# q and k kept in memory by half blocks, with the four chunks of a row side by side

## The reference

```python
xn = _layernorm(x)                                   # 6250 x 512
qkv = (xn @ W_qkv.T + b_qkv).reshape(1, S, 8, 192)   # 8 heads of 64
q, k, v = split(qkv, 3, axis=-1)
q, k = sigmoid(q), sigmoid(k)
i = sum(q * sum(k, axis=1), axis=3)                  # norms, a number per token and head
o = sum(k * sum(q, axis=1), axis=3)
i_hat = sum(q * sum(k / o, axis=1), axis=3)          # scales
o_hat = sum(k * sum(q / i, axis=1), axis=3)
vw = v * softmax(o_hat, axis=1)
kv = einsum('bshd,bshe->bsde', k, vw)                # per token: heads against heads
r = einsum('bshd,bsde->bshe', q / i, kv) * sigmoid(i_hat)
mix = r.reshape(1, S, 512) @ W_out.T + b_out
gnn = xn + relu(concat(xn, segment_mean(edge_attr, dst)) @ W1 + b1) @ W2 + b2
x = x + gnn + mix
x = x + gate * (_layernorm(x) @ We[best] + be[best])
```

## Time and profile before

| | |
|---|---|
| median of the runs | 2144.1 us |
| profiled execution | 2139.87 us, span 2138.1 us |
| TensorE busy | 1876.4 us, 88%, mean granted clock 0.919 |
| VectorE busy | 1223.4 us, 57% |
| ScalarE busy | 561.3 us, 26% |
| GpSimd busy | 1323.2 us, 62% |
| DMA | 530000 packets, 400.77 MB, mean 187 GB/s |
| hardware queue | 407780 packets, 60.7% of 16 engines |
| scatter queue | 119952 packets, 21.3% of 16 engines |

### The profile page before, as it was taken

The page is one execution under the profiler, slowest core; times in us unless marked ns, Lnnn a source line. Parts: engine busy times, 40 slices in busy tenths (PEclk is TensorE's granted clock), DMA queues, the critical chain, the costliest instruction groups (busy, mean ns, idle before and its releaser), DMA issues.

```text
span 2138.1 us, 31097 instructions
## 1 busy us (share of the span) xinstructions
PE 1876.4 (88%) x10776; PEld 1511.0 (71%) x10776; DVE 1223.4 (57%) x3872; ACT 561.3 (26%) x1314; POOL 1323.2 (62%) x850
## 2 busy tenths in 40 slices
PE   2799999999999999788765888878776999998798
PEld 1688888888888888544435777667664888887586
DVE  3643454443444332277755756566558888885575
ACT  1422333223333223111131221212122433343210
POOL 4888888888888888688888888888881000000100
PEclk9999999999999999866586988889887999999899
DMA  8977887877777677899799999999977766653884
GB/s 289 224 159 149 140 157 147 168 153 133 156 155 154 131 131 147 204 219 214 145 293 189 210 173 216 174 206 200 179 150 219 215 212 218 211 186 114 309 296 150
DMA packets 530000, 400.77 MB, mean 187 GB/s; under 512 B 356900, under 2 KB 394020, under 8 KB 529844
## 3 DMA queue, kind: packets, MB, share of 16 engines
q1 hardware_dynamic: 407780, 369.74, 60.7%
q0 software_dynamic: 119952, 28.99, 21.3%
q10 hardware_dynamic: 2112, 0.07, 0.1%
HBM read 244.05 MB, written 154.62 MB: 186 GB/s over the span
## 4 chain that ended last, share of the span: by engine, by line
PE 67%; SPq 17%; DVE 6%; DMA 5%; issue 3%; ACT 1%; POOL 0%; DVEq 0%; POOLq 0%; ACTq 0%
PE pr_out_bank L359 26%; PE gn_acc L359 12%; SPq L1333 8%; PE pr_v_bank L359 7%; PE edge_sum L243 6%; PE ex_y_bank L359 6%; SPq L1349 3%; PE at_acc L359 2%; PE nm_io_bank L854 1%; DVE nm_wide L1052 1%; SPq L190 1%; DMA done<-qk_T 1%; PE gn_h L1906 1%; DVE edge_sel L231 1%; PE gn_h L1907 1%
## 5 line engine op out<-in xcount | busy, mean ns | idle before, releaser
L291 POOL DMA_INDIRECT table<-edge_ring,edge_row x831 | 1312.0, 1579 | 292.7 <-issue 231.5
L231 DVE SCALAR_TENSOR_TENSOR edge_sel<-edge_dst_all,edge_dst_f,upper 128x128 f32<-128x128 int16 x831 | 317.4, 438 | 93.3 <-PE edge_sum L243 84.3
L359 PE MATMUL pr_out_bank<-pr_norm_xT_hi,pr_w_hi 128*128 128x512 f32 (+1 forms) x832 | 327.6, 394 | 0.0
L359 PE MATMUL pr_out_bank<-pr_norm_xT_lo,pr_w_hi 128*128 128x512 f32 (+1 forms) x832 | 319.3, 384 | 0.0
L359 PE MATMUL pr_out_bank<-pr_norm_xT_hi,pr_w_lo 128*128 128x512 f32 (+1 forms) x832 | 318.6, 383 | 0.0
L243 PEld LDWEIGHTS edge_sum<-edge_attr,edge_sel 128*128 128x128 f32 x1662 | 237.5, 213 | 112.1 <-DVE edge_sel L231 78.9
L243 PE MATMUL edge_sum<-edge_attr,edge_sel 128*128 128x65 f32 x1662 | 245.1, 297 | 74.6 <-DVE edge_sel L231 69.1
L2247 POOL DMA_INDIRECT ex_w_raw<-in_w_exp,ex_row x4 | 5.4, 1341 | 371.6 <-issue 371.6
L256 ACT ACTIVATE edge_ring<-edge_sum 128x260 f32<-128x260 f32 (+1 forms) x209 | 80.5, 385 | 408.3 <-PE edge_sum L243 320.7
L359 PEld LDWEIGHTS pr_out_bank<-pr_norm_xT_lo,pr_w_hi 128*128 128x128 f32 x832 | 156.6, 188 | 32.2
L359 PEld LDWEIGHTS pr_out_bank<-pr_norm_xT_hi,pr_w_lo 128*128 128x128 f32 x832 | 157.1, 189 | 28.3
(11 more groups left out here) (206 smaller groups left out, 3217.6 us busy)
## 6 DMA issues: line engine op xcount, KB each, us to landing
edge_dst_all<-dst SPq DMA_DIRECT2D x103, 256.0 KB
edge_attr<-in_edge_attr SPq DMA_DIRECT2D x103, 256.0 KB
qk_T<-pr_stage SPq DMA_DIRECT2D x48, 512.0 KB
h_pre_T<-pr_stage SPq DMA_DIRECT2D x48, 512.0 KB
gn_pre<-h_pre_T SPq DMA_DIRECT2D x48, 512.0 KB, 6.4
done<-qk_T SPq DMA_DIRECT2D x16, 1024.0 KB
table<-edge_ring,edge_row POOLq DMA_INDIRECT x831
pr_norm_x<-in_x SPq DMA_DIRECT2D x12, 1024.0 KB
```

What stands on the lines that cost most here:

```text
L231: op = dve.scalar_tensor_tensor(out=self.sel[q][0:rows, j, 0:rows], in0=self.dst_all[k][0:rows, t:t + m * (rows - 1) + 1:m], scalar=self.d ...
L291: pool.indirect_dma_start(self.c.table[t], bass.IndirectOffsetOnAxis(ap=self.row[k][0:rows, j:j + 1], axis=0), self.sums[k][0:rows, j, :], ...
L359: mm = pe.matmul(out, a, c, start=first and i == 0, stop=last and i == n - 1)
```

## The change

The memory behind q and k is `qk_halves` [2 sides, 25 half blocks, 128 features of a chunk, 4 chunks, 256 tokens] in place of `qk_T` [1024 features, 6250 tokens]. A feature row's four chunks of a half block lie side by side, 4 KB. A pair of chunks is stored as two runs of 2 KB per partition, at a pitch of 4 KB. Norms and scales load two runs of 4 KB per partition for q and as many for k. Attention loads two runs of 4 KB for each of 64 partitions, so that heads lie in SBUF in the order of parity, then chunk, and the matmul and the copy step over them in the order of heads. The number of DMAs is the same, but for the tail block of attention, which has four loads in place of two. The pair buffers and the blocks in SBUF hold half blocks one after the other, so ScalarE's sigmoid, VectorE's products and TensorE's head sums read or write a chunk in two pieces of 256.

```diff
+def by_half(ap):
+
+    return ap.rearrange("p (w t) -> p w t", w=2) if ap.shape[1] == BT else ap
...
+        pair_halves = [stage[:, i * PAIR:(i + 1) * PAIR].rearrange("p (w o t) -> p w o t", w=2, o=2) for i in range(RING)]
...
-                    sp.dma_start(kept[row:row + 2 * P, cols(b, n)].rearrange("(o p) t -> p o t", p=P),
-                                 pair[p % RING][:, :, 0:n]).then_inc(out_stored[p % RING], 16)
...
+                        if n == BT:
+                            sp.dma_start(c.qk[side, 2 * b:2 * b + 2, :, o:o + 2, :].rearrange("w p o t -> p w (o t)"),
+                                         pair_halves[p % RING].rearrange("p w o t -> p w (o t)")
+                                         ).then_inc(out_stored[p % RING], 16)
...
-                        act.activation(pair[p % RING][:, e % 2, 0:n], out_bank[e % 2][:, 0:n], ACT.Sigmoid,
+                        kept = pair_halves[p % RING][:, :, e % 2, :] if n == BT else pair_halves[p % RING][:, 0, e % 2, 0:n]
+                        act.activation(kept, by_half(out_bank[e % 2][:, 0:n]), ACT.Sigmoid,
...
+def chunks_of(flat, n):
+
+
+    if n == BT:
+        return flat.rearrange("p (w o t) -> p o w t", w=2, o=CH)
+    return flat[:, 0:CH * n].rearrange("p (o t) -> p o t", o=CH)
+
+
+def load_halves(sp, c, flat, side, b):
+
+
+
+    n = min(BT, TOKENS - b * BT)
+    if n == BT:
+        return sp.dma_start(flat.rearrange("p (w f) -> p w f", w=2),
+                            c.qk[side, 2 * b:2 * b + 2, :, :, :].rearrange("w p o t -> p w (o t)"))
+    return sp.dma_start(chunks_of(flat, n), c.qk[side, 2 * b, :, :, 0:n])
...
-            sp.dma_start(q[b % U][:, :, 0:sizes[b]], c.qk[0:DIM, block_at(b)].rearrange("(o p) t -> p o t", p=P)
-                         ).then_inc(q_in[b % U], 16)
+            load_halves(sp, c, q[b % U], 0, b).then_inc(q_in[b % U], 16)
...
-                x = q[b % U][:, o, 0:n] if o < CH else kept_block(c, b)[:, o - CH, :]
-                out = wide[(b * QK + o) % WIDE][:, 0:n]
+                x = chunks_of(q[b % U], n)[:, o] if o < CH else kept_block(c, b)[:, o - CH]
+                out = by_half(wide[(b * QK + o) % WIDE][:, 0:n])
...
-                for dst, row in ((q[b % 2], 0), (kk[b % 2], DIM)):
-                    at = b * BT + half * (BT // 2)
-                    sp.dma_start(dst[half * HDIM:(half + 1) * HDIM, :, 0:r],
-                                 c.qk[row:row + DIM, at:at + r].rearrange("(h d) t -> d h t", d=HDIM)
-                                 ).then_inc(qk_in[b % 2], 16)
+                for side, dst in enumerate((q[b % 2], kk[b % 2])):
+                    rows = slice(half * HDIM, (half + 1) * HDIM)
+                    if r == HALF:
+                        sp.dma_start(dst[rows, :, :].rearrange("d (x o) t -> d x (o t)", x=2),
+                                     c.qk[side, 2 * b + half, :, :, :].rearrange("(x d) o t -> d x (o t)", x=2)
+                                     ).then_inc(qk_in[b % 2], 16)
+                    else:
+                        for x in range(2):
+                            sp.dma_start(dst[rows, x * CH:(x + 1) * CH, 0:r],
+                                         c.qk[side, 2 * b, x * HDIM:(x + 1) * HDIM, :, 0:r]).then_inc(qk_in[b % 2], 16)
...
-                                       q[b % 2][rows, :, u * P + t:u * P + t + w].rearrange("d h t -> d t h"),
+                                       q[b % 2][rows, :, u * P + t:u * P + t + w].rearrange("d (x o) t -> d t o x", x=2),
...
-            act.activation(kt[u][0:rows, 0:r, :],
-                           kk[b % 2][0:rows, :, u * P:u * P + r].rearrange("d h t -> d t h"), ACT.Copy
+            act.activation(kt[u][0:rows, 0:r, :].rearrange("d t (o x) -> d t o x", x=2),
+                           kk[b % 2][0:rows, :, u * P:u * P + r].rearrange("d (x o) t -> d t o x", x=2), ACT.Copy
...
+        c.qk = nc.dram_tensor("qk_halves", [2, 2 * FULL + 1, P, CH, HALF], F32, kind="Internal").ap()
```

More of the change, by code:

```diff
@@ L26 @@
 BT = 512
+HALF = BT // 2
 FULL = TOKENS // BT
@@ L675, in body @@
                 for p in (2 * i, 2 * i + 1):
-                    kept, row = (c.qk, 2 * p * P) if p < CH else (c.h_pre, 2 * (p - CH) * P)
                     sp.wait_ge(out_free, b * OUTS + (2 * p + 2 + 2))
                     sp.sem_inc(c.passed, 1)
-                    sp.dma_start(kept[row:row + 2 * P, cols(b, n)].rearrange("(o p) t -> p o t", p=P),
-                                 pair[p % RING][:, :, 0:n]).then_inc(out_stored[p % RING], 16)
+                    if p >= CH:
+                        row = 2 * (p - CH) * P
+                        sp.dma_start(c.h_pre[row:row + 2 * P, cols(b, n)].rearrange("(o p) t -> p o t", p=P),
+                                     pair[p % RING][:, :, 0:n]).then_inc(out_stored[p % RING], 16)
+                    else:
+                        side, o = p // 2, p % 2 * 2
+                        if n == BT:
+                            sp.dma_start(c.qk[side, 2 * b:2 * b + 2, :, o:o + 2, :].rearrange("w p o t -> p w (o t)"),
+                                         pair_halves[p % RING].rearrange("p w o t -> p w (o t)")
+                                         ).then_inc(out_stored[p % RING], 16)
+                        else:
+                            sp.dma_start(c.qk[side, 2 * b, :, o:o + 2, 0:n], pair_halves[p % RING][:, 0, :, 0:n]
+                                         ).then_inc(out_stored[p % RING], 16)
         all_blocks(sp, 2, body)
@@ L873, in kept_block, with flat_block @@
     n = min(BT, TOKENS - b * BT)
-    return c.kept[:, b * CH * BT:b * CH * BT + CH * n].rearrange("p (o t) -> p o t", o=CH)
+    return chunks_of(c.kept[:, b * CH * BT:b * CH * BT + CH * n], n)
+def chunks_of(flat, n):
[8 more added lines that the diff above has]
+    return sp.dma_start(chunks_of(flat, n), c.qk[side, 2 * b, :, :, 0:n])
+def flat_block(c, b):
+    n = min(BT, TOKENS - b * BT)
+    return c.kept[:, b * CH * BT:b * CH * BT + CH * n]
 def norms_stage(nc, c, edges, before):
@@ L893, in norms_stage @@
         WIDE = 3
-        q = [c.done[:, u * CH * BT:(u + 1) * CH * BT].rearrange("p (o t) -> p o t", o=CH) for u in range(2)]
-        q += [sb(f"q{u}", [P, CH, BT]) for u in range(2, U)]
+        q = [c.done[:, u * CH * BT:(u + 1) * CH * BT] for u in range(2)]
+        q += [sb(f"q{u}", [P, CH * BT])[:, :] for u in range(2, U)]
         io = [sb(f"io{u}", [P, BT]) for u in range(2)]
@@ L937, in sums @@
                 pe.wait_ge(io_kept, b)
-            head_sums(pe, c, io_bank, [q[b % U][:, j, 0:n] for j in range(CH)],
-                      [kept_block(c, b)[:, j, :] for j in range(CH)], n).then_inc(io_mm, 1)
+            head_sums(pe, c, io_bank, [chunks_of(q[b % U], n)[:, j] for j in range(CH)],
+                      [kept_block(c, b)[:, j] for j in range(CH)], n).then_inc(io_mm, 1)
         def turn(b):
@@ L1138, in sums @@
                 pe.wait_ge(io_kept, b - 1)
-            head_sums(pe, c, io_bank[b % 2], [q[b % U][:, j, 0:n] for j in range(CH)],
-                      [kept_block(c, b)[:, j, :] for j in range(CH)], n).then_inc(io_mm, 1)
+            head_sums(pe, c, io_bank[b % 2], [chunks_of(q[b % U], n)[:, j] for j in range(CH)],
+                      [kept_block(c, b)[:, j] for j in range(CH)], n).then_inc(io_mm, 1)
         def turn(b):
@@ L1269, in attend_stage @@
         STEPS = 4
-        HALF = P // 2
+        NEAR = P // 2
         near = [[sb(f"near{g}_0", [P, 4, P])] for g in range(2)]
@@ L1315, in groups @@
             return []
-        t0 = step % 2 * HALF
-        return [(t, min(GT, subtiles(n)[sub] - t)) for t in range(t0, min(t0 + HALF, subtiles(n)[sub]), GT)]
+        t0 = step % 2 * NEAR
+        return [(t, min(GT, subtiles(n)[sub] - t)) for t in range(t0, min(t0 + NEAR, subtiles(n)[sub]), GT)]
     def landings(b, dmas=1):
@@ L1577, in neighbours @@
                 whole = len([g for g in gs if g[1] == GT])
-                at = (step // 2 + 2 * half) * (P // GT) + step % 2 * (HALF // GT)
+                at = (step // 2 + 2 * half) * (P // GT) + step % 2 * (NEAR // GT)
                 if whole:
```

9 lines of the change are left out of this document (4 added, 5 removed).

## The result

| | before | after |
|---|---|---|
| median, first comparison | 2143.16 us | 2131.73 us (2126.17 to 2134.24, 7 runs) |
| ratio | | 0.995, interval 0.9928 to 0.9972 |
| median, later comparison (after_again) | 2132.1 us | 2124.94 us (2116.92 to 2130.99, 12 runs) |
| ratio | | 0.9962, interval 0.9944 to 0.9981 |
| profiled execution (first) | 2139.87 us, span 2138.1 | 2126.26 us, span 2124.5 |

The change makes the kernel 0.4 to 0.5% faster, 8 to 11 us, and the forecast was 2131 us. Two of before's seven runs in the first comparison were in a slower state (2442.46 and 3568.3 us); they are in its median and left out of the ratio. The profiled execution of before lies 4 to 8 us over the medians of before in the later comparisons, so the 13.6 us between the two profiled executions overstate the change; the ratios are the measure.

A forecast was written before the change was run, and what follows sets the result against it. TensorE held 67% of the chain, sync-queue issuing 17%, with attention's mix loads queued behind q and k. Attention 7.0, scales 1.3 and norms 0.2 make 8.5 us off 2139.9: 2131 us (2119 to 2138), overall range 2086 to 2152.

The forecast's parts named there:

- The brake in attention is the partitions: Attention's q and k loads: half pace comes from filling 64 partitions per DMA, not from run length.
- the rise from 192 to 237 GB/s within one load: Attention's q and k load: rate rises where engines pass to the second partition half, run length unchanged; read as partitions.
- The zero that the prediction drew from it: Attention's q and k loads: by the skill's rule they already run at the 64-partition rate, so longer runs add 0.
- Attention's term: Attention's q and k loads: packet cost falls 84 to 79 ns a KB, 0.64 us a load, 11 loads, 7.0 us.
- Scales and norms: Loads there go from 2 to 4 KB runs: scales save 1.3 us, norms 0.2 us, only its first load counting.
- Stores and access patterns: Projection stores keep 2 KB runs; split or strided reads and writes by ScalarE, VectorE and TensorE cost nothing: 0.
- The slower rival, strided reads: Attention's reads of q and k get dearer from the 4 KB step; at double time 2173 us; chance 0.07.
- Mix loads stay blocked: Attention: the 15 mix loads stay issue-bound, the first still blocked for over 11 us.
- the rival in which fewer descriptors free the queue: Attention: mix loads get in early, 3 us for nine blocks, giving 2104 us; chance 0.08.
- Blocks were to be about 37 us apart: Attention: sign that the forecast is right, blocks following one another at about 37 us.
- The run-length rival: Attention's q and k loads: run length was the brake, 4 KB runs at 42 ns a KB, 2090 us; chance 0.2.
- That nothing arrives: Whole kernel: partitions alone set the pace, or long runs are cut into short packets, so 2139 us; chance 0.17.

The follow-up runs named there:

- after_again: The changed kernel itself, unaltered, run once more beside three other kernels on one chip: 2124.94 us, 0.9962 of the kernel before.
- attn_old_loads: The changed kernel, but attention loads runs of 1 KB as before, from another tensor of the old shape (other values): 2132.85 us, 0.9994 of before.
- wide_1k: The kernel before, 1 KB runs kept, but attention's q and k loads fill 128 partitions instead of 64 (values misplaced): 2072.14 us, 0.9718 of before.
- norms_old_loads: The changed kernel, but norms and scales load runs of 2 KB as before, from another tensor (other values): 2129.12 us, 0.9981 of before.
- wide_4k: The changed kernel, but each attention q or k load fills 128 partitions instead of 64 (values misplaced): 2067.62 us, 0.9688 of before.
- k_first: The changed kernel, but attention loads k of both half blocks, then q of both: 2115.56 us, 0.9927 of before.
- act_second_half: The changed kernel, but from block 2 on ScalarE's queue issues the second half block's q and k loads: 2131.06 us, 1.0003 of before.
- quarters_in_turn: The changed kernel, but eight 256 KB q and k loads per block, alternating partition halves, replace four of 512 KB: 2107.32 us, 0.9887 of before.

## Why the prediction was right

*The brake in attention is the partitions.* Shown, in both directions: with 128 partitions a KB takes 42 to 49 ns, with runs of 4 KB or of 1, in attention; with 64 it takes 77 to 84, and the scales' loads slow down alike when they are cut to 64. The sign that the prediction read, the rise from 192 to 237 GB/s within one load, pointed the right way and was thin, and there is some luck in that. In 1179 to 1181 only the hardware queue moved anything; in 1182 to 1183 it was

```profile
q1 hardware_dynamic: 220, 0.22, 97.6%
q0 software_dynamic: 73, 0.02, 20.0%
```

So the scatter queue had joined, and of the rise the hardware queue has 190 to 220 GB/s, over a single microsecond. The Trainium skill's rule (SBUF — State Buffer, Door 1: The DMA port swizzle) holds here: 369 to 212 GB/s is a factor of 1.7, and it gives 328 to 196. The zero that the prediction drew from it for the longer runs in attention lies just outside 6.8 give or take 5.4, and the packets' step from 84 to 77 ns a KB speaks against it.

*Attention's term: 5 ns a KB, 0.64 us a load, 7.0 us.* The traces give 84 to 77, 7 ns, 0.9 us a load and 9.9 us for eleven loads; the comparison of attn_old_loads with after_again gives 6.8 give or take 5.4. The term stands, a little small; whether all eleven loads pass on their whole 0.9 us is not resolved.

*Scales and norms: 1.3 and 0.2 us.* Together undersized, by the profiled executions. Three of them have the old loads in norms and scales (before, wide_1k, norms_old_loads) and seven the new ones (after, after_again, wide_4k, attn_old_loads, k_first, act_second_half, quarters_in_turn). Attention's first load is issued at 1096.6 to 1101.6, mean 1099.2, with the old ones and at 1093.4 to 1096.2, mean 1094.5, with the new: 4.7 us. From the first to the last of the scales' sums on k takes 44.5 to 45.7, mean 45.2, with the old and 42.3 to 44.2, mean 43.2, with the new: 2.0 us. So the scales' term of 1.3 is nearly right in size: a load's part of the chain there is about half a microsecond shorter (9.60 and 9.53 us before; 9.33, 9.03 and 8.49 after) where 1.7 ns a KB gave 0.11 each, but only some are on the chain. The other 2.7 us came in norms or ahead of them, where the prediction had 0.2, because it costed the first load alone and took the rest as hidden behind VectorE and TensorE. That is the term most likely to have failed, but it isn't shown: the last product of norms on k begins at 1052.0, 1049.5 and 1054.5 with the old loads and at 1047.5 to 1050.0 with the new, which overlap, and the difference of the ratios is 4 give or take 5.3. How shorter loads could act there, in a stretch with a DMA share of 0.87, stays open.

*Stores and access patterns: 0.* Shown for the operations (1951, 405 and 662 ns for 1957, 405 and 663) and for the projection's TensorE. The slower rival, strided reads, is out.

*Mix loads stay blocked.* 13.27 us for 12.69; the rival in which fewer descriptors free the queue is out. Blocks were to be about 37 us apart: the v loads at 1171.07 and, eight blocks on, 1464.08 give 36.6. The run-length rival (2090) is out by after itself, with 212 GB/s and not 300, and by wide_1k, which reached 2072 with the old runs. That nothing arrives is excluded narrowly, by 0.9972 and 0.9981.

*The total.* 8.5 us forecast; 10.7 and 8.1 measured. That the median also met 2131 owes something to the base: the first comparison's median of before was 2143, but 2132 to 2136 in the others, and the changed kernel took 2125 when it ran again. The difference is what the prediction got right.

## What to carry to other kernels

Ask of a slow DMA first how many partitions it fills and what its outermost dimension is, and only then how long its runs are: here the partitions were worth 3% of the kernel's time, the outermost dimension a factor of seven in rate (54 against 385 GB/s), and the longer runs 0.4 to 0.5%. A layout in memory is right for a load when the rows that go to all 128 partitions are one outermost dimension of it; where two stages want different partition orders, the one with the slower layout gives the gain back, so a second copy of the tensor, stored where the DMA queue has room, is the next thing to try (it was not tried here). A loading order that alternates between partition halves in small pieces gave 17.6 us, nearly a third of the 57 us that the wide loads gave over the changed kernel, with its layout as it was. Before crediting an order of loads with an earlier start of the consumer, look at what the consumer's semaphore waits for.

## What the runs showed that was not expected

- A load whose source has an outermost dimension of 2 ran on two engines, 12.6% of 16, and the kernel took 2522 us for 2125.
- A second queue didn't fill the other half beside the first: its loads came when the first had ended, and 85.5% for it left 6.8% for the first queue's small packets.
- k first gained 9.4 us, at the edge of the intervals, although ScalarE waits for all four loads: the halves alternate, and a packet takes 289.5 ns for 308 to 311.
- With 128 partitions the same matmuls of attention took 13 us less TensorE time, at a granted clock of 0.90 for 0.86, on top of 46 us less idle time.
- The layout that gave attention 64.5 us took back 41.5 ahead of it, where 5 to 25 were expected.
